# A two-layer windowed transformer: half of a turned input moved to the next step, and one keys' product moved into the projection

## The chip, the cores and the metric

The kernel runs on one core of a Trainium2 chip. The metric is the device time of one execution in microseconds, from start to end of the program. TensorE (PE in the rows) multiplies, DVE is the vector engine, ACT the scalar engine, POOL is GpSimd, SP issues transfers.

## The reference

Eight images of 56 x 56 with 16 channels pass a ReLU and nine 9 x 9 filters each, which gives 160 channels per pixel. Then come two transformer blocks with windows of 7 x 7 pixels and 5 heads of 32, the second with windows shifted by 3 and a mask. A linear layer, a synthesis filter and a 1 x 1 convolution end it. All is float32.

```
for i, (shift, mask) in enumerate(zip(SHIFTS, (None, MASK1))):
    x3 = _swin_block(x3, shift, mask, ...)

# in _swin_block
x = _ln(x, ln1g, ln1b)                       # roll and window partition if shift
q, k, v = split(x @ qkvw + qkvb)
attn = softmax(q @ k.T * HEAD_DIM ** -0.5 + bias + mask)
x = sc + (attn @ v) @ projw + projb
h = _ln(x, ln2g, ln2b)
return x + gelu(h @ w1 + b1) @ w2 + b2
```

## The kernel before

Three phases run one after the other: `phase_a` filters the images, `phase_b` computes both blocks and the linear layer, `phase_c` ends. The change lies in `phase_b`, some 2900 us of the span.

`phase_b` works on strips of 14 rows (two rows of windows), four per image, 32 per layer. Its body is executed once per step `i`, 0 to 63, and once more as prologue and as tail. It is a software pipeline of three strips: attention of strip `i` (parameter `la`, its layer), the MLP of strip `m = i - 1` (`lm`), and the front, that is layer norm and the products Q, K, V, of strip `i + 1` (`ln`). A step with `lm` 0 is called a layer 0 step here (32 of them), one with `lm` 1 a layer 1 step (31, and the tail). Layer 1 steps also compute the last linear layer. Each engine has its own copy of the body, written out by hand, and executes it strictly in that order; semaphores tie them.

Every float32 operand of a matrix product is split in a high part, made by ACT, and a low part, made by DVE as the difference; `split_passes` then multiplies four times (L118). The products of a step, by the names of their uses:

- `T1A0, T1C0, T1A1, T1C1`: TensorE turns the normalised strip z1 (columns 0 to 127 as A, the rest as C; half 0 has four tiles, half 1 three; L1328). `Q0, K0, B0, Q1, K1, B1`: queries, keys, and the fifth head's queries and keys, for halves 0 and 1 of the strip. `V0` to `V3`: values. ACT copies each out; `fifth_head` takes four copies.
- S0 to S3: scores (L1387) of four groups of windows; DVE adds the bias (L1168), takes the maximum (L1175) and the difference (L1178); ACT the exponentials (L997). `OT0` to `OT3`: attention's outputs turned, split by ACT (L1009) and DVE (L1203). `P0, P1, P2`: the projection, of 1, 3 and 3 tiles; DVE adds the residual.
- `T2A0, T2C0, T2A1, T2C1`: z2, the second layer norm's output, turned (L1328) for the MLP, split by `t_hi` on ACT (L1031) and `t_lo` on DVE (L1215) into z2t. `G0` to `G9`: the MLP's first product, five feature blocks for half 0 of the strip, then five for half 1; ACT's gelu (L1040) frees the bank. `W0` to `W5`: its second product (L1441); DVE adds x1b (L1229). `L0` to `L3`: the linear layer from z2t, scaled out by ACT (L1022).

PSUM has two rings whose uses take the banks in turn: `ra` with three banks and `rm` with two. A product waits until the reader has freed the use that had its bank before. A `Ring` is a list of uses in order; the rings PRO, RA and END serve the prologue, the steps and the last step.

TensorE's order at the end of a step was: W3 (layer 1: W4), K1, a wait for OT3's split, P0, P1, B1, P2, V2, S0 of the next strip, W4 and W5 (layer 1: W5, then L0 to L3), T2A0 and T2C0, V3, T2A1 and T2C1. The next step begins with G0 to G4, S1, G5 to G9, S2, W0, T1A0 and T1C0.

DVE's order there: residuals 0 and 1, their statistics and `variance` of half 0, residual 2, `normalise` of half 0 of z2 (L1123), statistics, W4's addition (layer 0), variance of half 1, W5's addition, `normalise` of half 1, `t_lo(0)`, `t_lo(1)`. Next step: the statistics of the strip xa (L1100), the scores' operations for groups 0 and 1, `normalise` of z1.

POOL's body, which the change leaves as it is: `inv_std`, the deviation of the coming strip (L898, eleven small operations); `repeat_rest(z1)` (L904), which copies the rest columns of z1 twice and releases T1; for each half of z2 a power (L928), then `repeat_rest(z2)` (L904), which releases T2 of that half; in layer 1 the linear part's addition to yz (L923); last x1b, in layer 0 seven additions (L936), in layer 1 two passes over the strip (L940, L943).

SP loads the strips xa and xr, and stores xo (layer 0, after W5) or yz (layer 1, after POOL's L923).

Of the kernel before, what the change touches and what calls it, by code (L numbers as in the profile page):

```python
# [17 lines left out]
F32 = mybir.dt.float32  # L18
# [618 lines left out]
def phase_b(nc, keep, xs0, xs1, ys):  # L637
    with ExitStack() as ctx:
# [6 lines left out]
        def bank(name):  # L645
# [53 lines left out]
        FRONT = ["T1A0", "T1C0", "T1A1", "T1C1", "Q0", "K0", "B0", "V0", "Q1", "V1", "K1", "B1", "V2", "V3"]  # L699
        PRO = Ring(FRONT, 3, {})  # L700
        RA = Ring(["T1A0", "T1C0", "T1A1", "T1C1", "OT0", "Q0", "K0", "OT1", "B0", "V0", "Q1", "OT2", "V1", "OT3", "K1",
                   "P0", "P1", "B1", "P2", "V2", "V3"], 3, {})
        END = Ring(["OT0", "OT1", "OT2", "OT3", "P0", "P1", "P2"], 3, {})
# [65 lines left out]
        def t2_half_freed(i, lm):  # L769

            return rm_free[1], m_before(i, lm, M_USES) - 1
# [179 lines left out]
        def _(act):  # L951
            act_ = nc.scalar.activation

            def body(i, la, lm, ln):
# [23 lines left out]
                def fifth_head(hf):  # L978
                    use = f"B{hf}"
                    act.wait_ge(*a_full(i, use))  # L980
                    dims = [[2 * WQ, 4], [1, WT]]
                    for p in range(2):
                        act_(view(q4, p * WP, HD, hf * QH + p * WQ, dims), view(bank_a(i, use), 0, HD, p * WQ, dims), ACT.Copy,
                             scale=float(HD) ** -0.5)
                        last = act_(view(k4, p * WP, HD, hf * QH + p * WQ, dims), view(bank_a(i, use), HD, HD, p * WQ, dims),
                                    ACT.Copy)
                    last.then_inc(a_freed(i, use)[0], 1)

                def values(j):
                    use = f"V{j}"  # L990
                    act.wait_ge(*a_full(i, use))
                    act_(view(vb, 0, QP, j * VJ, [[VW, 2 * HEADS], [1, HD]]),
                         view(bank_a(i, use), 0, QP, 0, [[HD, 2 * HEADS], [1, HD]]), ACT.Copy).then_inc(a_freed(i, use)[0], 1)
# [32 lines left out]
                def t_hi(hf):  # L1026
                    t0, nt = HALF[hf]
                    for part, dst, rows in (("A", z2t[0], 128), ("C", z2t[2], CR)):
                        use = f"T2{part}{hf}"
                        act.wait_ge(*m_full(i, lm, use))  # L1030
                        act_(dst[0:rows, t0 * TT:(t0 + nt) * TT], bank_m(i, lm, use)[0:rows, 0:nt * TT],  # L1031
                             ACT.Copy).then_inc(s_hi2, 1)

                if lm is not None:
                    for g in range(2 * FT):
# [5 lines left out]
                             ACT.Gelu_apprx_tanh).then_inc(m_freed(i, lm, use)[0], 1)  # L1041
                if la is not None:
# [21 lines left out]
                if ln is not None:  # L1064
                    fifth_head(0)
                    values(0)
# [6 lines left out]
                if ln is not None:  # L1073
                    values(1)
# [20 lines left out]
        def _(dve):  # L1095
# [45 lines left out]
            def body(i, la, lm, ln):  # L1141
# [66 lines left out]
                def t_lo(hf):  # L1208
                    t0, nt = HALF[hf]
                    cols = slice(t0 * TT, (t0 + nt) * TT)  # L1210
                    for n, (part, dst, src, rows) in enumerate((("A", z2t[1], z2t[0], slice(0, 128)),
                                                               ("C", z2t[2], z2t[2], slice(REST, 2 * REST)))):
                        use = f"T2{part}{hf}"
                        dve.wait_ge(s_hi2, hi2(i, 2 * hf + n + 1))
                        v.tensor_tensor(dst[rows, cols], bank_m(i, lm, use)[rows, 0:nt * TT], src[rows, cols].bitcast(F32),  # L1215
                                        ALU.subtract).then_inc(m_freed(i, lm, use)[0], 1)
# [60 lines left out]
                if la is not None:  # L1277
# [19 lines left out]
                    residual(2)  # L1297
                    dve.wait_ge(s_pow, 2 * i + 1)
                    normalise(1, z2, x1, *HALF[0])
                    x1_stats(2, True)  # L1300
                if lm == 0:
                    mlp_out(4)
                if la is not None:
                    variance(i, 1)
                if lm is not None:
                    mlp_out(5)
                if la is not None:
                    dve.wait_ge(s_pow, 2 * i + 2)
                    normalise(1, z2, x1, *HALF[1])
                    t_lo(0)  # L1310
                    t_lo(1)
# [5 lines left out]
        def _(pe):  # L1317
# [13 lines left out]
            def body(i, la, lm, ln):  # L1331
# [135 lines left out]
                def mlp_turned(z, name, hf):  # L1467
# [402 lines left out]
```

## Time and profile before

| | us |
|---|---|
| median of 3 runs | 3453.58 |
| lowest, highest | 3445.36, 3461.8 |
| profiled execution | 3450.4 |
| its span, first to last instruction | 3448.9 |
| TensorE busy | 3213.2 (93%) |
| DVE, ACT, POOL busy | 2133.2 (62%), 1779.8 (52%), 908.5 (26%) |
| mean granted TensorE clock | 0.958 |

A row of a timeline has the start and the duration in us, the engine, the line, what is written and read, the shape, the number of instructions merged, and in brackets the idle time before with what ended it. The granted clock is the share of full speed that TensorE was allowed; its two levels are 1.2 and 2.4 GHz. A busy TensorE is not necessarily at its peak.

### The profile page before, as it was taken

The page shows a single profiled execution, that of the slowest core. Times are in us where ns is not written, and L with a number is a line of the kernel's source. Part 1 is how long each engine was busy: PE and PEld are TensorE (multiplying, and loading weights), DVE is VectorE, ACT ScalarE, POOL GpSimd, SP SyncE. Part 2 cuts the span into 40 slices and gives each one's busy share as a digit, 9 for nine tenths or more (in the row PEclk, how much of TensorE's full clock was granted, in tenths as well). Part 3 has the DMA queues.
Part 4 walks back from the last instruction along what each step waited for, and adds up shares of the span by engine and source line. Part 5 has one row for each costly group of instructions (what it writes and reads, how often), then busy time and mean ns, then how long its engine had stood idle before and what let it go on. Part 6 is the DMA issues. An engine that isn't in the chain of part 4 may idle for free. (4 is left out here: it accounts for less than half of the span.)

```text
span 3448.9 us, 103586 instructions
## 1 busy us (share of the span) xinstructions
PE 3213.2 (93%) x40530; PEld 2876.9 (83%) x40530; DVE 2133.2 (62%) x6493; ACT 1779.8 (52%) x4297; POOL 908.5 (26%) x1432
## 2 busy tenths in 40 slices
PE   7996999999999999999999999999999999999689
PEld 6884888888888888888888888888888888888589
DVE  1114677777777777777766666666666666666232
ACT  1111555555555555555555555555656556655221
POOL 5300222222222222222222233322333223332111
PEclk9996899999999999999999999999999999999789
DMA  5321111111111111111111111111111111111275
GB/s 103 94 74 43 30 36 35 35 35 35 35 35 35 35 35 35 35 35 45 44 39 25 36 36 36 30 25 34 36 36 36 28 25 36 36 36 24 51 137 94
DMA packets 246678, 148.38 MB, mean 43 GB/s; under 512 B 31729, under 2 KB 246068, under 8 KB 246586
## 3 DMA queue, kind: packets, MB, share of 16 engines
q1 hardware_dynamic: 244882, 146.95, 18.5%
q0 software_dynamic: 1728, 0.48, 0.1%
q8 instruction: 49, 0.80, 0.1%
q14 instruction: 19, 0.16, 0.0%
HBM read 96.74 MB, written 52.50 MB: 43 GB/s over the span
## 5 line engine op out<-in xcount | busy, mean ns | idle before, releaser
L1441 PE MATMUL rm<-w,ht 128*112 128x160 f32 x4480 | 683.8, 303 | 0.0
L1441 PEld LDWEIGHTS rm<-w,ht 128*112 128x112 f32 x4480 | 610.1, 177 | 9.6 <-ACT ht L1040 0.2
L928 POOL TENSOR_TENSOR rs<-ln_tmp,mhalf 112x4 f32<-112x4 f32 (+1 forms) x128 | 118.9, 929 | 1663.6 <-DVE ln_tmp L1119 1663.6
L1040 ACT ACTIVATE ht<-rm 128x448 f32<-128x448 f32 (+1 forms) x640 | 319.2, 499 | 233.8 <-PE rm L118 231.9
L118 PE MATMUL rm<-z2t_hi,w_hi 128*128 128x448 f32 (+1 forms) x640 | 267.6, 418 | 35.3 <-DVE z2t_lo L1215 34.6
L1168 DVE TENSOR_TENSOR sc<-so,tabs 113x490 f32<-113x490 f32 x256 | 171.2, 669 | 141.2 <-PE so L1387 139.1
L118 PE MATMUL rm<-z2t_lo,w_hi 128*128 128x448 f32 (+1 forms) x640 | 229.2, 358 | 0.0
L118 PE MATMUL rm<-z2t_rest,w_rest 98*128 98x448 f32 (+1 forms) x640 | 228.4, 357 | 0.0
L118 PE MATMUL rm<-z2t_hi,w_lo 128*128 128x448 f32 (+1 forms) x640 | 228.3, 357 | 0.0
L904 POOL TENSOR_TENSOR z<-z,one 112x448 f32<-112x448 f32 (+2 forms) x192 | 131.6, 685 | 367.1 <-DVE z L1123 367.1
L118 PEld LDWEIGHTS rm<-z2t_hi,w_hi 128*128 128x128 f32 x640 | 128.0, 200 | 109.9 <-ACT ht L1040 51.0
L1178 DVE TENSOR_TENSOR sm<-sc,mx 113x490 f32<-113x490 f32 x256 | 174.0, 680 | 37.1 <-ACT pr L997 25.4
L1408 PEld LDWEIGHTS so<-vb,pt 49*49 49x49 f32 x10240 | 142.8, 123 | 60.4 <-issue 55.0
L1328 PE MATMUL rm<-ident,z 112*128 112x112 f32 (+1 forms) x896 | 144.1, 292 | 48.5 <-POOL z L904 32.7
L1185 DVE RECIPROCAL rd<-so 113x10 f32<-113x10 f32 x256 | 56.6, 221 | 208.9 <-PE so L1408 201.1
L1123 DVE TENSOR_SCALAR z<-x,mean,rs 112x160 f32<-112x160 f32 x448 | 133.8, 360 | 80.9 <-POOL rs L928 80.9
L1387 PEld LDWEIGHTS so<-kt,qm 64*49 64x49 f32 x8192 | 141.0, 122 | 49.6 <-issue 44.0
L1009 ACT ACTIVATE ot_hi<-ra 128x98 fp32r<-128x98 f32 x512 | 103.0, 261 | 149.8 <-PE ra L1420 149.8
L1387 PE MATMUL so<-kt,qm 64*49 64x49 f32 x8192 | 172.8, 208 | 1.6 <-DVE sc L1168 1.6
L969 ACT ACTIVATE qm<-ra,qpair 128x400 f32<-128x400 f32 x256 | 138.2, 591 | 69.6 <-PE ra L118 69.6
L1175 DVE TENSOR_REDUCE mx<-sc 113x10 f32<-113x490 f32 x256 | 169.3, 661 | 6.6
L1408 PE MATMUL so<-vb,pt 49*49 49x33 f32 x10240 | 170.3, 210 | 2.8 <-issue 0.9
(244 smaller groups left out, 9300.9 us busy)
## 6 DMA issues: line engine op xcount, KB each, us to landing
xa<-xs SPq DMA_DIRECT2D x128, 245.0 KB
xr<-xs SPq DMA_DIRECT2D x128, 245.0 KB
xs<-a_tok SPq DMA_DIRECT2D x8, 1960.0 KB, 9.5
xs<-xo SPq DMA_DIRECT2D x64, 245.0 KB
ys<-yz SPq DMA_DIRECT2D x64, 245.0 KB
c_y<-ys SPq DMA_DIRECT2D x48, 260.0 KB
c_y<-ys SPq DMA_DIRECT2D x16, 280.0 KB
c_taps<-in_f_syn SPq DMA_DIRECT2D x24, 126.0 KB, 5.1
```

The lines of the kernel that those rows point to most:

```text
L118: last = nc.tensor.matmul(out, lhs, rhs, start=(n == 0), stop=(n == len(pairs) - 1))
L904: gp.tensor_tensor(view(t, 0, TT, t0 * ZW + DIM, [[ZW, nt], [REST, 2], [1, REST]]), once, view(one, 0, TT, 0, [[0, nt], [0, 2], [0, REST]] ...
L969: last = act_(qm[:, odd * QN + hf * QH:odd * QN + (hf + 1) * QH], bank_a(i, use)[:, 0:QH], ACT.Copy, scale=keep.qpair[:, odd:odd + 1])
L1040: act_(ht[:, f * SN + t0 * TT:f * SN + (t0 + nt) * TT], bank_m(i, lm, use)[:, 0:nt * TT], ACT.Gelu_apprx_tanh).then_inc(m_freed(i, lm, use ...
L1123: ins = v.tensor_scalar(z[:, t * ZW:t * ZW + DIM], x_[:, t * DIM:(t + 1) * DIM], mean[n][:, t:t + 1], rs[n][:, t:t + 1], ALU.subtract, ALU ...
L1168: v.tensor_tensor(view(sc, 0, QP, 0, [[SX, 2], [1, SX]]), view(so, 0, QP, 0, [[512, 2], [1, SX]]), tab, ALU.add).then_inc(s_sadd, 1)
L1175: v.tensor_reduce(mx[:], s3, AX.X, ALU.max).then_inc(s_smax, 1)
L1178: v.tensor_tensor(sm[j % 2][:].rearrange("q (g k) -> q g k", k=WT), s3, view(mx, 0, QP, 0, [[1, 2 * HEADS], [0, WT]]), ALU.subtract).then_ ...
L1328: last = tr(bank_of(use)[0:rows, t * TT:(t + 1) * TT], z[:, c:c + rows], keep.ident[0:TT, 0:TT])
L1387: last = mm(so[w * WP:w * WP + WT, row * 512 + b * WT:row * 512 + (b + 1) * WT], q, k, start=True, stop=True)
L1408: last = mm(so[w * WP:w * WP + WT, p * 512 + OC + h * VW:p * 512 + OC + (h + 1) * VW], pt[p * WP:p * WP + WT, h * GK + w * WT:h * GK + (w ...
L1441: last = mm(bank_m(i, lm, use)[0:TT, t * DIM:(t + 1) * DIM], ht[:, c:c + TT], keep.w["w2", lm][:, f * DIM:(f + 1) * DIM], start=(f == 0), ...
```

## The change

Three things. (1) The second half of turned z2 (T2A1, T2C1) is no longer made at the end of step `i`, but in step `i + 1` between G2 and G3, in the `ra` ring instead of `rm`. ACT splits it after gelu G2, DVE after adding the bias of score group 0; TensorE waits for both splits ahead of G5. (2) K1 moves from before P0 to between P1 and P2. (3) B1 goes behind V3 at the end of the step; its copies and V3's go to ACT's next step, behind gelu G2 and gelu G0. Besides, the product W4 (layer 1: W5) and its addition move ahead of V2, and on DVE ahead of the normalisation of half 0, while `t_lo` of half 0 now stands ahead of the normalisation of half 1, not behind it. POOL and SP are unchanged.

```diff
-        RA = Ring([..., "V1", "OT3", "K1",
-                   "P0", "P1", "B1", "P2", "V2", "V3"], 3, {})
+        RA = Ring([..., "V1", "OT3",
+                   "P0", "P1", "K1", "P2", "V2", "V3", "B1", "T2A1", "T2C1"], 3, {})
-        T2 = ["T2A0", "T2C0", "T2A1", "T2C1"]
+        T2 = ["T2A0", "T2C0"]
...
-            return rm_free[1], m_before(i, lm, M_USES) - 1
+            return rm_free[1], m_before(i, lm, M_USES)
+        def turned_full(i, lm, use):
+            return m_full(i, lm, use) if use[-1] == "0" else a_full(i, use)
... ACT
                              ACT.Gelu_apprx_tanh).then_inc(m_freed(i, lm, use)[0], 1)
+                        if g == 0 and la is not None:
+                            values(3, i - 1)
+                        if g == 2:
+                            t_hi(m, 1)
+                            if la is not None:
+                                fifth_head(1, i - 1)
...
                     keys(1)
-                    fifth_head(1)
-                    values(2)
+                    values(2, i)
...
                 if la is not None:
-                    t_hi(0)
-                if ln is not None:
-                    values(3)
-                if la is not None:
-                    t_hi(1)
+                    t_hi(i, 0)
... DVE
                     scores_biased(0, i, la)
+                if lm is not None:
+                    t_lo(m, 1)
+                if la is not None:
                     scores_less_max(0, i)
...
                     residual(2)
+                if lm is not None:
+                    mlp_out(4 + lm)
+                if la is not None:
                     dve.wait_ge(s_pow, 2 * i + 1)
                     normalise(1, z2, x1, *HALF[0])
                     x1_stats(2, True)
                 if lm == 0:
-                    mlp_out(4)
+                    mlp_out(5)
                 if la is not None:
                     variance(i, 1)
-                if lm is not None:
-                    mlp_out(5)
-                if la is not None:
+                    t_lo(i, 0)
                     dve.wait_ge(s_pow, 2 * i + 2)
                     normalise(1, z2, x1, *HALF[1])
-                    t_lo(0)
-                    t_lo(1)
... TensorE
                     pe.wait_ge(*t2_half_freed(i, lm))
-                    mlp_in(range(FT))
+                    mlp_in(range(3))
+                    pe.wait_ge(s_z[1], 2 * m + 2)
+                    mlp_turned(m, 1)
+                    mlp_in(range(3, FT))
                 if la is not None:
                     scores(1, i)
                 if lm is not None:
+                    pe.wait_ge(*a_freed(m, "T2A1"))
+                    pe.wait_ge(*a_freed(m, "T2C1"))
                     mlp_in(range(FT, 2 * FT))
...
-                if ln is not None:
-                    front_product("K", 1)
                 if la is not None:
                     pe.wait_ge(*a_freed(i, "OT3"))
                     projection(0)
                     projection(1)
                 if ln is not None:
-                    front_product("B", 1)
+                    front_product("K", 1)
                 if la is not None:
                     projection(2)
+                if lm is not None:
+                    mlp_out(4 + lm)
                 if ln is not None:
                     values(2)
                     scores(0, i + 1)
                 if lm == 0:
-                    mlp_out(4)
-                if lm is not None:
                     mlp_out(5)
                 if lm == 1:
                     linear(range(4))
                 if la is not None:
                     pe.wait_ge(s_z[1], 2 * i + 1)
-                    mlp_turned(z2, "T2", 0)
+                    mlp_turned(i, 0)
                 if ln is not None:
                     values(3)
-                if la is not None:
-                    pe.wait_ge(s_z[1], 2 * i + 2)
-                    mlp_turned(z2, "T2", 1)
+                    front_product("B", 1)
```

## Rows read from the trace of the kernel before

**Rows 1.** The page, first part: busy time, share of the span and instructions of each engine.

```profile
PE 3213.2 (93%) x40530; PEld 2876.9 (83%) x40530; DVE 2133.2 (62%) x6493; ACT 1779.8 (52%) x4297; POOL 908.5 (26%) x1432
```

**Rows 2.** Windows: 30 layer 0 steps, 27 layer 1 steps, three single steps, the kernel's start.

```profile
core 0: us, PE busy (x) PEld busy (x) DVE busy (x) ACT busy (x) POOL busy (x), PEclk, DMA share, GB/s
422.34:1714.68 1292.34, 1241.73 (x17340) 1111.12 (x17341) 942.85 (x2971) 758.10 (x1861) 322.12 (x661) 0.99 0.15 36
1852.41:3132.89 1280.48, 1229.30 (x16363) 1106.44 (x16363) 859.54 (x2701) 747.29 (x1864) 394.75 (x487) 0.96 0.14 32
1498.17:1542.21 44.04, 42.36 (x579) 38.16 (x579) 31.43 (x100) 25.28 (x63) 10.72 (x23) 0.96 0.14 34
1542.21:1584.98 42.77, 41.09 (x578) 36.69 (x578) 31.42 (x100) 25.26 (x63) 10.71 (x23) 1.00 0.14 35
...
2896.29:2942.65 46.36, 44.37 (x606) 39.67 (x606) 31.83 (x100) 27.64 (x70) 14.61 (x19) 1.00 0.13 33
341.50:352.20 10.70, 7.25 (x96) 6.56 (x100) 6.70 (x16) 4.62 (x12) 0.93 (x1) 0.52 0.22 48
```

**Rows 3.** Waits of TensorE in the 30 layer 0 steps: total us, times, longest.

```profile
PE rm L1328 <- POOL z L904: 27.9, 30, 0.9
PE rm L118 <- DVE z2t_lo L1215: 17.2, 30, 0.7
```

**Rows 4.** Waits of TensorE in the 27 layer 1 steps, the longest in total.

```profile
PE rm L118 <- DVE yz L1229: 28.1, 27, 1.0
```

**Rows 5.** Timeline of a layer 0 step where the projection begins: start us, us.

```profile
1529.00 0.46 PE L118 MATMUL ra<-z1t_hi,qkv_hi 128*128 128x400 f32 x1
1529.09 0.42 DVE L1203 TENSOR_TENSOR ot_rest<-ra,ot_rest 32x98 fp32r<-32x98 f32 x2
...
1529.86 0.24 PE L118 MATMUL ra<-proj_hi,ot_hi 128*112 128x160 f32 x1
```

**Rows 6.** Timeline of TensorE, end of that step: T2A0, G0, G5.

```profile
1537.62 0.55 PE L1328 MATMUL rm<-ident,z 112*128 112x112 f32 x4
...
1542.21 0.47 PE L118 MATMUL rm<-z2t_hi,w_hi 128*128 128x448 f32 x1 [0.58 <-DVE z2t_lo L1215]
...
1547.36 0.42 PE L118 MATMUL rm<-z2t_hi,w_hi 128*128 128x336 f32 x1
```

**Rows 7.** Groups of instructions of ACT: one of the fifth head's two kinds of copy.

```profile
L983 ACT ACTIVATE q<-ra 32x196 f32<-32x196 f32 x256 | 82.0, 320 | 116.2 <-PE ra L118 114.7
```

**Rows 8.** Timeline of a layer 1 step's end: L1 to L3 out, T2A0, split of T2C0, G0.

```profile
2937.65 1.79 ACT L1022 ACTIVATE xo<-rm,std 112x160 f32<-112x160 f32 x5 [1.22 <-PE rm L118]
...
2939.16 0.99 PE L1328 MATMUL rm<-ident,z 112*128 112x112 f32 x8 [0.16 <-ACT xo L1022]
...
2941.04 0.62 DVE L1215 TENSOR_TENSOR z2t_rest<-rm,z2t_rest 32x448 fp32r<-32x448 f32 x1
...
2942.65 0.47 PE L118 MATMUL rm<-z2t_hi,w_hi 128*128 128x448 f32 x1 [0.45 <-DVE z2t_lo L1215]
```

**Rows 9.** Timeline of the same step: DVE's second normalisation, POOL's chain, T1.

```profile
2937.27 0.91 DVE L1123 TENSOR_SCALAR z<-x,mean,rs 112x160 f32<-112x160 f32 x3 [0.73 <-POOL rs L928]
...
2938.26 0.51 POOL L904 TENSOR_TENSOR z<-z,one 112x192 f32<-112x192 f32 x1 [1.02 <-DVE z L1123]
2939.58 2.57 POOL L923 TENSOR_TENSOR yz<-yz,xo 112x1120 f32<-112x1120 f32 x1 [0.81 <-ACT xo L1022]
...
2946.80 0.97 POOL L898 TENSOR_TENSOR ln_tmp<-st 112x7 f32<-112x7 f32 x3
...
2952.79 0.94 POOL L904 TENSOR_TENSOR z<-z,one 112x448 f32<-112x448 f32 x1 [2.12 <-DVE z L1123]
...
2954.99 0.93 PE L1328 MATMUL ra<-ident,z 112*128 112x112 f32 x8
```

**Rows 10.** Timeline of DVE and POOL in the last step with attention.

```profile
3182.68 2.60 POOL L943 TENSOR_TENSOR x1b<-x1b,b 112x1120 f32<-112x1120 f32 x1
...
3183.32 2.49 DVE L1178 TENSOR_TENSOR sm<-sc,mx 113x490 f32<-113x490 f32 x1
```

**Rows 11.** Timeline of TensorE at the kernel's first turn T1 after attention begins.

```profile
344.19 1.75 PE L1328 MATMUL ra<-ident,z 112*128 112x112 f32 x8 [3.45 <-POOL z L904]
...
347.64 1.06 PE L1408 MATMUL so<-vb,pt 49*49 49x33 f32 x40 [0.76 <-ACT pt L1002]
```

More of the change, by code:

```diff
@@ L976, in keys, with fifth_head, values @@
                     act_(kt[:, hf * QH:(hf + 1) * QH], bank_a(i, use)[:, 0:QH], ACT.Copy).then_inc(a_freed(i, use)[0], 1)
[L978 removed]
+                def fifth_head(hf, n):
                     use = f"B{hf}"
[L980 removed]
+                    act.wait_ge(*a_full(n, use))
                     dims = [[2 * WQ, 4], [1, WT]]
                     for p in range(2):
[L983 removed]
+                        act_(view(q4, p * WP, HD, hf * QH + p * WQ, dims), view(bank_a(n, use), 0, HD, p * WQ, dims), ACT.Copy,
                              scale=float(HD) ** -0.5)
[L985 removed]
+                        last = act_(view(k4, p * WP, HD, hf * QH + p * WQ, dims), view(bank_a(n, use), HD, HD, p * WQ, dims),
                                     ACT.Copy)
[L987 to L989 removed]
+                    last.then_inc(a_freed(n, use)[0], 1)
+                def values(j, n):
                     use = f"V{j}"
[L991 removed]
+                    act.wait_ge(*a_full(n, use))
                     act_(view(vb, 0, QP, j * VJ, [[VW, 2 * HEADS], [1, HD]]),
[L993 removed]
+                         view(bank_a(n, use), 0, QP, 0, [[HD, 2 * HEADS], [1, HD]]), ACT.Copy).then_inc(a_freed(n, use)[0], 1)
                 def exps(j):
@@ L1029, in t_hi @@
                         use = f"T2{part}{hf}"
-                        act.wait_ge(*m_full(i, lm, use))
-                        act_(dst[0:rows, t0 * TT:(t0 + nt) * TT], bank_m(i, lm, use)[0:rows, 0:nt * TT],
+                        act.wait_ge(*turned_full(n, lm, use))
+                        act_(dst[0:rows, t0 * TT:(t0 + nt) * TT], turned_bank(n, lm, use)[0:rows, 0:nt * TT],
                              ACT.Copy).then_inc(s_hi2, 1)
@@ L1041, in body @@
                              ACT.Gelu_apprx_tanh).then_inc(m_freed(i, lm, use)[0], 1)
+                        if g == 0 and la is not None:
[4 more added lines that the diff above has]
+                                fifth_head(1, i - 1)
+                elif la is not None:
+                    values(3, i - 1)
+                    fifth_head(1, i - 1)
                 if la is not None:
@@ L1064, in body @@
                 if ln is not None:
[L1065 to L1066 removed]
+                    fifth_head(0, i)
+                    values(0, i)
                 if la is not None:
@@ L1206, in outputs_lo, with t_lo @@
                     ins.then_inc(a_freed(i, use)[0], 1)
-                def t_lo(hf):
+                def t_lo(n, hf):
                     t0, nt = HALF[hf]
                     cols = slice(t0 * TT, (t0 + nt) * TT)
-                    for n, (part, dst, src, rows) in enumerate((("A", z2t[1], z2t[0], slice(0, 128)),
+                    for k, (part, dst, src, rows) in enumerate((("A", z2t[1], z2t[0], slice(0, 128)),
                                                                ("C", z2t[2], z2t[2], slice(REST, 2 * REST)))):
                         use = f"T2{part}{hf}"
-                        dve.wait_ge(s_hi2, hi2(i, 2 * hf + n + 1))
-                        v.tensor_tensor(dst[rows, cols], bank_m(i, lm, use)[rows, 0:nt * TT], src[rows, cols].bitcast(F32),
-                                        ALU.subtract).then_inc(m_freed(i, lm, use)[0], 1)
+                        dve.wait_ge(s_hi2, hi2(n, 2 * hf + k + 1))
+                        v.tensor_tensor(dst[rows, cols], turned_bank(n, lm, use)[rows, 0:nt * TT], src[rows, cols].bitcast(F32),
+                                        ALU.subtract).then_inc(turned_freed(n, lm, use)[0], 1)
                 def mlp_out(n):
```

19 lines of the change are left out of this document (12 added, 7 removed).

## The prediction

> **What bounds the kernel now.** The page comes first: TensorE is busy for 93% of the span and no other engine for over 62% [rows 1], so a microsecond counts where TensorE waits. The windows by stage come next. Thirty layer 0 steps take 1292.34 us, 43.08 each, but one at the full granted clock takes 42.77 and one in which the clock fell takes 44.04; 27 layer 1 steps take 1280.48 us, 47.43 each, against 46.36 at the full clock [rows 2]. So the falls cost 1292.34 - 30 x 42.77 = 9 us in layer 0 and about 1.06 a step in layer 1. The waits of TensorE show three per step and all stand at the step's end [rows 3, 4]: layer 0 waits 0.93 for z2's second half from POOL, 0.57 for its split by DVE and a little for DVE's last addition; layer 1 waits 1.04 for DVE's addition of W5, then a little for ACT's linear copies and for the split. The rest is a chain without gaps.
>
> The change attacks these waits. What matters is what becomes late instead, so I walked one step of each layer through the new orders, engine by engine, with the durations of the timeline (the rows shown are those that carry the sum). Times are those of the step of before; an event "earlier by 1" is so against that step.
>
> **Layer 0.** The start of the projection loses its cover. TensorE ends W3 at 1529.00 and now wants P0 at once; but P0 waits for the split of OT3, which DVE ends at 1529.09 + 0.42 = 1529.51 [rows 5]. K1, 0.86 us long (1529.00 to 1529.86), hid that. P0 starts at 1529.57: a new stall of 0.57, and P0 only 0.29 earlier. From P0 to T2A0 there were 7.76 us (1529.86 to 1537.62); B1 (0.75) leaves and K1 (0.86) enters, so T2A0 stands at 1537.44. DVE's addition of W5 now comes ahead of the second variance: 1537.62 to 1537.94, and T2C0, which needs its bank, starts at 1538.0. Variance 0.83 to 1538.8, the two splits 0.62 each with their small gaps to 1540.1, no longer behind a normalisation of 0.91. TensorE comes from V3 and B1 at 1539.96. G0 starts at 1540.15 instead of 1542.21 [rows 6], 2.06 earlier. Then 0.63 is given back for the six transposes that now stand between G2 and G3; their input is ready at about 1541.7, behind G0 to G2. ACT pays next: after gelu G2 (to 1543.4) it does two splits of 0.45, then the fifth head, four copies of 0.32 to 0.33 [rows 7], to 1545.6, and only then gelu G3 (0.55), which frees G5's bank at 1546.15. TensorE is done with S1 0.5 before. V3's copy hides in ACT's wait for G1. G5 starts at 1546.2 instead of 1547.36. The new wait for T2C1's split ahead of G5 costs nothing: DVE ends it near 1544.9, before S1's end at 1545.7. On DVE the first max and difference of the scores queue behind that split, some 1 us later, and ACT wants them only after its last gelu, past 1550. Nor does POOL come late: its residual additions and statistics bring z1 by 1551.9, and T1 wants it at 1554.42 - 1.15 = 1553.27. So a layer 0 step saves **1.15 us**, 32 of them 37 us. The stalls that remain (0.57, some 0.3, 0.2 and 0.5) lie apart, so I also credit the 9 us of clock falls: -46 in all. Bounds: no credit for the clock and half the gain, -18; the stall at G5 hidden, -62.
>
> **Layer 1, TensorE.** P0 is again 0.29 earlier. W5 is computed and added before the linear layer, so the 1.04 wait for L1 goes. Next late is ACT: each pair of linear tiles takes it 0.68 to 0.72, and with L0 at 2934.34 its five remaining tiles end near 2938.42 instead of 2937.65 + 1.79 = 2939.44. T2A0 starts at 2938.15 instead of 2939.16. Its splits end 1.0 earlier too, at 2940.65 instead of 2941.04 + 0.62 [rows 8], and G0 starts at 2940.72 instead of 2942.65. The same 0.63 and the same wait at G5 follow. TensorE would come to T1 (the turn of z1) at 2954.99 - 1.07 = 2953.9.
>
> **Layer 1, POOL.** Here is the step that I think decides. DVE used to normalise z2's second half at 2937.27, while it waited for T2; now that stands behind the first half's splits, so it starts at 2940.69, 3.42 later. POOL, in its own order, repeats the rest columns of that half (2938.26, now 2941.68), and only then adds the linear part (2.57), makes x1b in two passes (both done by 2946.85) and computes the next strip's deviation (2946.80 to about 2950.7), after which DVE normalises z1 (2.00) and POOL finishes it (2952.79 to 2953.73) [rows 9]. Nothing in that chain had to wait: its only slack was the 0.81 before the linear addition, at 2939.58, and the time from 2953.73 to T1 at 2954.99, which less 0.12 for the semaphore (2940.50 in layer 0's counterpart to its release) leaves 1.14. The addition now starts at 2942.15, **2.57 later**. Without any other effect z1 is turned at 2953.85 + 2.57 = 2956.42, 1.43 later than before. After T1 the step is TensorE's own chain, back to P0, so all of it lengthens the step. (SP stores yz behind the linear addition, so 2.6 later; DVE needs that buffer again with W0's addition, over 8 us on, and xr's load, queued behind the store, is needed half a step later.)
>
> Two corrections have only bounds. POOL's deviation now took 0.97 for three operations of 0.2 each because DVE's L1178 ran over them [rows 9]; without that the chain is 0.43 shorter, a shift of 1.0. The other way, the passes over x1b move to where DVE has both of its L1178 of the step. One L1178 of the trace lasted 2.49 us instead of 0.67, while POOL's L943 ran from 3182.68 to 3185.28 [rows 10]. If both L1178 go between POOL's passes, 2 x 0.67 is added to the 1.0: 2.34. I take the middle, **1.7**, for a step of 48.1 at the full clock, with TensorE standing still for some 2.8 us ahead of T1. The Trainium skill (SBUF — State Buffer, Who interferes with whom) says that a DVE instruction with two SBUF inputs and a GpSimd instruction that reads SBUF exclude each other for a whole instruction, whoever came first; the trace agrees, with the 2.49 us. By that rule alone the shift is 2.34, and the sum below would be 31 x 0.64 = 20 us higher.
>
> **The clock.** A standstill of 2.8 us in one piece is more than any steady step has now; falls came after pieces of 0.93 and 0.57 close together, or of 1.04. After the 3.45 us that TensorE waited for z at the same place in the kernel's first step, the clock was 0.52 from 341.50 to 352.20, that is half, and the eight transposes of T1 took 1.75 instead of 0.93 [rows 2, 11]. From 344.19 to 352.20 there are 8.0 us, 0.76 of them waiting; 7.25 us of work at a rate of 0.53 lose 3.4. So the price of a fall there is up to 3.4; in a layer 0 step it was 1.27 [rows 2]. It may be 0, if none comes. I take **2.0 a step** as a mean over nearly every step having one, nearer to the seen prices than to the largest, as TensorE's half-speed time partly lies in the wait.
>
> **The sum.** Layer 1: 48.1 + 2.0 = 50.1 against 47.43, +2.65 on 31 steps = +82. Layer 0: -46. First and last steps: the same work, taken at nothing (under 3 us either way). 3450.4 + 36 = 3486, made against the profiled execution, which took 3450.4 us around a span of 3448.9; the median of the runs is 3 us above it: **3490 us**, 1.1% slower. A measurement of this kernel tells about 0.5% from no change, 3436 to 3471.
>
> **Rivals.** (1) The clock holds, or falls as seldom as now: 3450.4 - 46 + 31 x 0.67 = 3425, 3428 as a median, faster. For it: idle stretches of 1.0 to 1.6 us per step mostly cost nothing now. Against it: the first steps' fall. It decides when the clock's price in layer 1 is under about 0.3 a step. Chance 0.18, of which some reaches into no change. (2) POOL's chain does not bind, because something in it is shorter than I read it; then layer 1 takes 46.36 - 1.07 = 45.3 without falls, and the total is 3450 - 46 - 66 = 3338. This needs z1 to be 2.1 us earlier than the mildest bound, against durations that repeat to hundredths in every step: 0.07. (3) Both bounds at their worst (2.34, 3.4) and layer 0 gaining only 18: 3450 - 18 + 31 x 4.7 = 3578, or beyond if the low clock lasts: 0.08. (4) The gains and losses cancel, since the price of the clock is near 1 a step: 3455. The waits are moved, and nothing comes of the change: 0.10. The forecast itself, 3471 to 3560, has 0.57.
>
> With these, faster 0.22, no change 0.15, slower 0.63. The range of 8 in 10 is 3415 to 3565: it takes in the forecast, the cancelling case and most of the first rival, and leaves out the second and the worst of the third.
>
> **What the changed profile would show.** Right: no wait of TensorE for POOL's z and DVE's split at the end of layer 0 steps; a wait of about 0.57 before P0 in both layers; 0.3 to 0.6 before G5 for ACT; layer 0 steps of 41.6 us; in layer 1, TensorE's turn of z1 into the ra banks waiting 2 to 3.5 us for POOL L904 in each step, POOL's linear addition starting 2.5 us later against P0, no wait for DVE before L1, and a granted clock under 0.96 in that layer, low just after T1. Wrong: layer 1 steps below 47 us, or a clock near 1.00 there. If layer 0 does not gain, ACT's fifth head or the cover of P0 is what I mis-sized.

## The result and the profile after

The change made the kernel slightly slower: a median of 3465.85 us over six executions (3463.76 to 3474.78) against 3452.18 over six of the kernel before (3444.56 to 3461.8). The ratio is 1.0048 with a 95% interval of [1.0027, 1.0069]: small, but the interval leaves out 1. The forecast was 3490 us, a step of +36 to +38; the measured one is +14.

| | before | after |
|---|---|---|
| profiled execution, us | 3450.4 | 3464.7 |
| its span | 3448.9 | 3462.9 |
| mean granted TensorE clock | 0.958 | 0.961 |

The page of the kernel after, its first part:

```profile
PE 3195.4 (92%) x40530; PEld 2866.0 (83%) x40530; DVE 2158.6 (62%) x6493; ACT 1740.5 (50%) x4297; POOL 921.5 (27%) x1432
```

The same instructions ran, and TensorE is busy 17.8 us less than in [rows 1]. Little can be seen in such a mean, since the two layers went opposite ways. Windows of the kernel after, each from a P0 (the projection's start) to a P0: 32 layer 0 steps, 29 layer 1 steps, one layer 0 step, two layer 1 steps, and 7 us around the start of T1 in the last of them (2616.95). Columns as in [rows 2].

```profile
365.36:1691.32 1325.96, 1300.76 (x18477) 1171.27 (x18477) 1005.16 (x3166) 788.14 (x1984) 349.41 (x704) 1.00 0.15 37
1734.65:3188.96 1454.31, 1333.59 (x17574) 1197.78 (x17575) 948.34 (x2901) 785.50 (x2001) 432.39 (x522) 0.96 0.13 30
1028.30:1069.73 41.43, 40.67 (x578) 36.63 (x579) 31.43 (x100) 24.63 (x62) 10.93 (x22) 1.00 0.14 36
2339.76:2387.97 48.21, 44.04 (x607) 39.50 (x607) 32.70 (x101) 26.92 (x69) 14.91 (x18) 1.00 0.13 32
2588.18:2639.33 51.15, 46.98 (x607) 42.23 (x607) 32.69 (x101) 27.17 (x69) 14.90 (x18) 0.93 0.13 30
2616.00:2623.00 7.00, 6.04 (x59) 5.69 (x63) 3.69 (x7) 2.24 (x4) 0.82 (x1) 0.53 0.35 72
```

And the kernel before, cut at the same places (P0 of the same steps), which [rows 2] are not:

```profile
364.63:1745.13 1380.50, 1324.62 (x18476) 1185.34 (x18477) 1005.19 (x3166) 808.07 (x1984) 343.86 (x704) 0.99 0.14 36
1790.56:3166.66 1376.10, 1320.86 (x17576) 1189.18 (x17574) 923.26 (x2901) 802.73 (x2001) 423.63 (x522) 0.96 0.14 32
```

So layer 0 gained 54.5 us (43.14 to 41.44 a step) and layer 1 lost 78.2 (47.45 to 50.15 a step). A layer 1 step takes 48.21 where the clock held, and 51.15 in the one shown where it fell: there the granted clock is 0.53, near half speed, in the 7 us that begin 0.95 before the wait for z1 ends, and the eight transposes of T1 take 1.75 instead of 0.98. 23 of the 29 steps are longer than 48.35. Of the rest of the difference, the step between the two stretches gained 2.1 (45.43 to 43.33), the last step with attention 0.85 (44.97 to 44.12), and everything behind it 7.45 (3448.9 - 3211.63 = 237.27 to 3462.9 - 3233.08 = 229.82); the start lost 0.7. The sum is -54.5 + 78.2 - 2.1 - 0.85 - 7.45 + 0.7 = +14.0, the difference of the spans. The last 0.7 says nothing: in the profiles of the versions below, whose order up to there is that of the kernel after, the first P0 comes anywhere from 360.43 to 374.29.

Waits of TensorE after, layer 0 stretch (columns as in [rows 3]). The two at the step's end of [rows 3] are gone; the one before P0 and the one before G5 are new:

```profile
PE ra L118 <- DVE ot_rest L1216: 13.4, 33, 1.7
PE rm L118 <- ACT ht L1049: 11.4, 32, 0.4
```

Layer 1 stretch, against [rows 4]:

```profile
PE ra L1343 <- POOL z L913: 83.1, 29, 2.9
PE rm L1343 <- ACT xo L1031: 11.0, 29, 0.5
PE ra L118 <- DVE ot_rest L1216: 10.7, 29, 0.4
PE rm L118 <- ACT ht L1049: 10.1, 29, 0.4
```

83.1 us are waited at the turn of z1, 2.86 in each of 29 steps. The timeline of the layer 1 step from 2339.76 shows how it comes about. DVE:

```profile
2351.17 0.62 DVE L1228 TENSOR_TENSOR z2t_lo<-rm,z2t_hi 128x448 fp32r<-128x448 f32 x1 [3.23 <-ACT z2t_hi L1040]
2351.82 0.62 DVE L1228 TENSOR_TENSOR z2t_rest<-rm,z2t_rest 32x448 fp32r<-32x448 f32 x1
2352.48 0.91 DVE L1136 TENSOR_SCALAR z<-x,mean,rs 112x160 f32<-112x160 f32 x3
...
2358.11 0.97 DVE L1191 TENSOR_TENSOR sm<-sc,mx 113x490 f32<-113x490 f32 x1
...
2360.58 1.48 DVE L1191 TENSOR_TENSOR sm<-sc,mx 113x490 f32<-113x490 f32 x1
...
2365.39 2.00 DVE L1136 TENSOR_SCALAR z<-xa,mean,rs 112x160 f32<-112x160 f32 x7 [3.33 <-POOL rs L907]
```

POOL, in the same stretch:

```profile
2348.01 0.85 POOL L937 TENSOR_TENSOR rs<-ln_tmp,mhalf 112x3 f32<-112x3 f32 x1 [0.96 <-DVE ln_tmp L1132]
2353.46 0.51 POOL L913 TENSOR_TENSOR z<-z,one 112x192 f32<-112x192 f32 x1 [4.60 <-DVE z L1136]
2353.93 2.61 POOL L932 TENSOR_TENSOR yz<-yz,xo 112x1120 f32<-112x1120 f32 x1
2356.48 2.07 POOL L949 TENSOR_TENSOR x1b<-lin_sum,mean 112x1120 f32<-112x1120 f32 x1
2358.63 2.90 POOL L952 TENSOR_TENSOR x1b<-x1b,b 112x1120 f32<-112x1120 f32 x1
2361.49 0.97 POOL L907 TENSOR_TENSOR ln_tmp<-st 112x7 f32<-112x7 f32 x3
...
2367.48 0.93 POOL L913 TENSOR_TENSOR z<-z,one 112x448 f32<-112x448 f32 x1 [2.12 <-DVE z L1136]
```

TensorE:

```profile
2368.54 0.98 PE L1343 MATMUL ra<-ident,z 112*128 112x112 f32 x8 [2.86 <-POOL z L913]
```

The half layer norm's power, which L1136 needs, is ready at 2348.86. DVE then stands idle for 3.23, waiting for ACT, since a split stands before the normalisation in its order. POOL in its turn stands idle for 4.60. From there to 2368.41 POOL works, or waits for DVE's L1136, which itself waits for POOL's statistics: the chain that the prediction followed in [rows 9]. The linear addition (now L932) starts 14.17 after P0 instead of 2939.58 - 2928.22 = 11.36 (2928.22 is P0 of that step in the trace of before), that is 2.81 later.

### The profile page after: what moved, and what is told of

It reads as the page before. It is cut to its first block and busy times, and to the rows that moved or that the text cites. A ratio compares the mean times of both kernels' runs of the same rounds, so it can differ in the third digit from the quotient of the medians.

```text
span 3462.9 us, 104230 instructions
## 1 busy us (share of the span) xinstructions
PE 3195.4 (92%) x40530; PEld 2866.0 (83%) x40530; DVE 2158.6 (62%) x6493; ACT 1740.5 (50%) x4297; POOL 921.5 (27%) x1432
## 5 line engine op out<-in xcount | busy, mean ns | idle before, releaser
L1456 PE MATMUL rm<-w,ht 128*112 128x160 f32 x4480 | 715.6, 311 | 0.0
L1456 PEld LDWEIGHTS rm<-w,ht 128*112 128x112 f32 x4480 | 636.8, 183 | 8.0 <-ACT ht L1049 0.2
L1343 PE MATMUL ra<-ident,z 112*128 112x112 f32 (+1 forms) x1280 | 176.0, 281 | 109.2 <-POOL z L913 109.2
L1343 PEld LDWEIGHTS ra<-ident,z 112*128 112x128 f32 (+1 forms) x1280 | 142.9, 144 | 125.3 <-issue 112.9
L971 ACT ACTIVATE z1t_hi<-ra 128x448 fp32r<-128x448 f32 (+1 forms) x128 | 68.2, 533 | 308.8 <-PE ra L1343 308.8
L1191 DVE TENSOR_TENSOR sm<-sc,mx 113x490 f32<-113x490 f32 x256 | 205.6, 803 | 16.3 <-ACT pr L1006 1.0
L1181 DVE TENSOR_TENSOR sc<-so,tabs 113x490 f32<-113x490 f32 x256 | 170.9, 668 | 53.7 <-PE so L1402 45.1
L1001 ACT ACTIVATE vb<-ra 113x320 f32<-113x320 f32 x256 | 112.8, 441 | 179.6 <-PE ra L118 178.1
L1136 DVE TENSOR_SCALAR z<-xa,mean,rs 112x160 f32<-112x160 f32 x448 | 128.1, 358 | 113.8 <-POOL rs L907 113.8
L985 ACT ACTIVATE kt<-ra 128x400 f32<-128x400 f32 x128 | 64.6, 504 | 244.1 <-PE ra L118 244.1
L1411 PE MATMUL pt_ps<-gather,pr 113*128 113x113 f32 x1280 | 181.2, 275 | 0.7 <-ACT pr L1006 0.7
```

Source lines behind the costliest of these rows:

```text
L1136: ins = v.tensor_scalar(z[:, t * ZW:t * ZW + DIM], x_[:, t * DIM:(t + 1) * DIM], mean[n][:, t:t + 1], rs[n][:, t:t + 1], ALU.subtract, ALU ...
L1181: v.tensor_tensor(view(sc, 0, QP, 0, [[SX, 2], [1, SX]]), view(so, 0, QP, 0, [[512, 2], [1, SX]]), tab, ALU.add).then_inc(s_sadd, 1)
L1191: v.tensor_tensor(sm[j % 2][:].rearrange("q (g k) -> q g k", k=WT), s3, view(mx, 0, QP, 0, [[1, 2 * HEADS], [0, WT]]), ALU.subtract).then_ ...
L1343: last = tr(bank_of(use)[0:rows, t * TT:(t + 1) * TT], z[:, c:c + rows], keep.ident[0:TT, 0:TT])
L1411: last = tr(pt_ps[:, h * GK:h * GK + QP], pr[j % 2][:, SLOT[h] * 2 * WP:(SLOT[h] + 1) * 2 * WP], gather[:])
L1456: last = mm(bank_m(i, lm, use)[0:TT, t * DIM:(t + 1) * DIM], ht[:, c:c + TT], keep.w["w2", lm][:, f * DIM:(f + 1) * DIM], start=(f == 0), ...
```

## The experiments

The theory (A): z1 comes late because L1136 of z2's second half stands behind the first half's split on DVE, which is DVE's order alone; the wait that follows in turn costs clock. Rivals: POOL's chain is too long whatever DVE does (port conflicts with DVE, or x1b itself); or the clock falls because of the many new gaps of all the engines' queues, not because of that one wait. The two with the normalisation first, the one with 17 products and K1 alone ran on one chip, beside 16 executions of the kernel before with a median of 3451.63; the other four on another, beside 7 with 3454.46. Ratios are to these.

**The normalisation first, in layer 1 only.** From the changed kernel, on DVE:

```diff
                     variance(i, 1)
-                    t_lo(i, 0)
+                    if lm != 1:
+                        t_lo(i, 0)
                     dve.wait_ge(s_pow, 2 * i + 2)
                     normalise(1, z2, x1, *HALF[1])
+                    if lm == 1:
+                        t_lo(i, 0)
```

> The changed kernel, with one edit: in layer 1 steps DVE normalises z2's second half before it splits the turned first half, as in the kernel before. Theory A (POOL's chain is late because of that normalisation's place, and the clock falls because TensorE stands still ahead of T1): the wait of 2.86 us for POOL's z goes, POOL's linear addition then starts at ACT's last linear copy, and the step at the full clock falls from 48.2 to about 45.4 us; no falls are left in layer 1, so 29 steps of 50.15 become 45.4 and the total drops by about 135 us, to some 3330. Theory B (the chain is bound by something else, the shared port or ACT's linear copies): POOL's chain starts at most 1 us earlier, the wait keeps over half of its length, total 3400 to 3450. Theory C (the falls have another cause than the standstill): step 45.4 at the full clock, but a granted clock of still about 0.96 in layer 1, total about 3390.

3321.75 us (3313.76 to 3326.93), ratio 0.9634 [0.9605, 0.9663]: 144 us below the median of the kernel after. One layer 1 step and 28 of them in its windows:

```profile
2456.38:2501.51 45.13, 43.84 (x606) 39.52 (x607) 31.76 (x101) 26.92 (x69) 14.58 (x18) 1.00 0.15 34
1779.38:3043.10 1263.72, 1227.36 (x16968) 1106.79 (x16969) 889.56 (x2801) 753.67 (x1932) 408.38 (x504) 1.00 0.14 34
```

Every layer 1 step takes 45.13, the clock is 1.00 throughout, and the waits of TensorE in these 28 steps no longer hold POOL's z:

```profile
PE rm L1346 <- ACT xo L1031: 10.6, 28, 0.4
PE ra L118 <- DVE ot_rest L1216: 10.4, 28, 0.4
PE rm L118 <- ACT ht L1049: 9.8, 28, 0.4
```

POOL in the step from 2456.38:

```profile
2464.62 0.85 POOL L937 TENSOR_TENSOR rs<-ln_tmp,mhalf 112x3 f32<-112x3 f32 x1 [0.95 <-DVE ln_tmp L1132]
2466.50 0.51 POOL L913 TENSOR_TENSOR z<-z,one 112x192 f32<-112x192 f32 x1 [1.02 <-DVE z L1136]
2466.97 2.58 POOL L932 TENSOR_TENSOR yz<-yz,xo 112x1120 f32<-112x1120 f32 x1
...
2471.64 2.60 POOL L952 TENSOR_TENSOR x1b<-x1b,b 112x1120 f32<-112x1120 f32 x1
```

The linear addition starts 10.59 after P0 instead of 14.17. So the chain moved up by 3.58, more than the wait of 2.86, and its length didn't bind. The first part of (A) stands: the order on DVE alone cost 48.20 - 45.13 = 3.07 a step at the full clock, and 1.95 more through the clock. The swap of the two lines, not the move of the second half of z2, is what made this change a loss.

**The same swap in both layers.**

```diff
                     variance(i, 1)
-                    t_lo(i, 0)
                     dve.wait_ge(s_pow, 2 * i + 2)
                     normalise(1, z2, x1, *HALF[1])
+                    t_lo(i, 0)
```

> The changed kernel with the same edit in both layers. Theory A expects layer 1 as in the run beside it. In layer 0, DVE has the second variance behind W5's addition, so the normalisation waits for POOL's power and the splits of the turned first half come about 1.8 us later; G0 is then late by 1.5 to 1.9 us, and the layer 0 step goes from 41.43 to 43.0 to 43.3, at or above the 42.77 of the kernel before: total some 50 to 60 us above the run with the edit in layer 1 alone. The rival, that the order on DVE costs nothing in layer 0, because G0's wait moves into waits that are there anyway: step of 41.4 to 41.8.

3417.98 us (3415.95 to 3425.74), 0.9913 [0.9889, 0.9937], so 96 us worse than with the swap in layer 1 alone. Layer 1 is as good (45.1); layer 0, in 32 steps, is

```profile
374.29:1792.88 1418.59, 1340.49 (x18476) 1202.73 (x18476) 1007.43 (x3166) 788.94 (x1984) 331.56 (x704) 0.97 0.14 35
```

44.33 a step instead of 41.44. Its largest wait of TensorE, and where it comes from on DVE in one step:

```profile
PE rm L118 <- DVE z2t_rest L1228: 53.8, 32, 1.7
```

```profile
916.67 0.91 DVE L1136 TENSOR_SCALAR z<-x,mean,rs 112x160 f32<-112x160 f32 x3 [0.97 <-POOL rs L937]
917.49 0.62 DVE L1228 TENSOR_TENSOR z2t_lo<-rm,z2t_hi 128x448 fp32r<-128x448 f32 x1
918.14 0.62 DVE L1228 TENSOR_TENSOR z2t_rest<-rm,z2t_rest 32x448 fp32r<-32x448 f32 x1
```

Here there is no linear layer between the variance and T2, so DVE waits 0.97 for POOL's power and spends 0.91 while G0 already wants the split. G0 waits 1.69 in every step. At the full clock the step is 43.31, 1.88 longer; the clock, which fell in 24 of 32 steps, adds 1.0 on the mean. The same two lines are right in one order in layer 0 and in the other in layer 1.

**The wait kept, but filled with work.** To separate the clock from the wait, layer 1 steps of the changed kernel compute products that no result uses while z1 is still on its way:

```diff
                     mlp_out(0)
+                if lm == 1 and la is not None and ln is not None:
+                    pe.wait_ge(s_pte, i * NG)
+                    for n in range(17):
+                        mm(pt_ps[0:TT, 0:DIM], ht[:, 0:TT], keep.w["w2", lm][:, 0:DIM], start=True, stop=True)
                 if ln is not None:
                     front_turned(0)
```

> The changed kernel, with work added that no result uses: in layer 1 steps, between W0 and the turn of z1, TensorE multiplies 17 more times as in W0, about 2.4 us, into a bank that is free. Theory A (the falls of the clock come from the standstill): the wait for POOL's z shrinks to about 0.5 us, the clock in layer 1 stays at 1.00, every such step takes 48.2 to 48.3 instead of 50.15, and the whole kernel is about 55 us faster than the changed one, in spite of more work: some 3410. Theory C (the falls have another cause, such as the thin products behind the turn): clock still about 0.96, steps of about 50.2, total as the changed kernel or above.

3460.53 us (3454.07 to 3465.43), 1.0027 [1.0004, 1.0051]. The total was missed, and the trace says why: each product is two instructions, and the 34 take longer than the wait they were to fill.

```profile
2319.91 4.78 PE L1505 MATMUL pt_ps<-w,ht 128*112 128x160 f32 x34
2324.53 0.93 PE L1343 MATMUL ra<-ident,z 112*128 112x112 f32 x8
```

T1 starts 4.62 behind the first of them, where the wait had been 2.86. It comes 30.38 after P0 instead of 28.78, so the step is 49.76 at the full clock. The clock itself answers the question: 1.00 over the 28 steps. With ten products instead of 17:

> The changed kernel with 10 products of work that no result uses in place of 17. The run before gave each product two instructions of 0.14 us on TensorE, so 17 took 4.6 us, more than the wait of 2.86 they were to fill; 10 take 2.75. The falls of the clock were gone with 17 (none in layer 1, 23 in the changed kernel). If the standstill is their cause, they stay away and the step is the one at the full clock, 48.2 us, which is 1.9 below the changed kernel's mean of 50.15 on 29 steps: total about 55 us below the changed kernel, 3410. If only the larger amount of work kept them away, falls come back and the total is 3440 to 3465.

Three executions took 3406.22, 3409.16 and 3419.37 us, a ratio of 0.9878 [0.9838, 0.9918]. A fourth took 4761.92 at a mean granted clock of 0.599; it has no profile, and why stays open. Window of 28 layer 1 steps, and T1 of one:

```profile
1780.15:3129.80 1349.65, 1309.38 (x17529) 1181.69 (x17529) 915.40 (x2801) 753.71 (x1932) 417.01 (x504) 1.00 0.14 31
```

```profile
2336.13 2.88 PE L1505 MATMUL pt_ps<-w,ht 128*112 128x160 f32 x20
2339.13 0.98 PE L1343 MATMUL ra<-ident,z 112*128 112x112 f32 x8
```

T1 comes when it did (28.77 after P0), the step is the 48.20 of a step without a fall, and there is no fall: 1349.65 / 28 = 48.20. Against the changed kernel 50.15 - 48.20 = 1.95 a step are gone by giving TensorE more to do. Every other engine's order and z1's time are as they were, so the new gaps in the other queues are not the cause. That settles the second part of (A): it is TensorE's standstill before T1 that the clock answers to, and its price was 1.95 a step on the mean, 57 us in 29 steps.

**K1 moved alone.** From the kernel before, K1 goes between P1 and B1, and nothing else changes:

```diff
-        RA = Ring([..., "OT3", "K1",
-                   "P0", "P1", "B1", "P2", "V2", "V3"], 3, {})
+        RA = Ring([..., "OT3",
+                   "P0", "P1", "K1", "B1", "P2", "V2", "V3"], 3, {})
...
-                if ln is not None:
-                    front_product("K", 1)
                 if la is not None:
                     pe.wait_ge(*a_freed(i, "OT3"))
...
                 if ln is not None:
+                    front_product("K", 1)
                     front_product("B", 1)
```

> The kernel before, with one part of the change alone: K1 between P1 and P2, ahead of B1. My theory: the cover of P0 is gone, TensorE waits 0.37 us for the split of OT3 in every step, as in the changed kernel; nothing is won, since z2's second half at the step's end hangs on DVE and POOL, which come 0.4 to 0.5 us earlier with P0 and P1 but 0.1 to 0.4 later with P2: layer 0 step 42.5 to 43.1 against 42.77, layer 1 46.4 to 46.8 against 46.37, total within 15 us of the kernel before. The rival, that starting the projection earlier is the gain of the change: steps shorter by 0.4 or more in both layers, total 3425 or less.

3440.48 us (3429.89 to 3448.06), 0.9966 [0.9949, 0.9983]: 11 us faster than before, a step as small as that of the whole change, the other way. In layer 1 it helps (46.17 a step without falls, against 47.45 with them in 11 of 29), as the wait for yz shrinks from [rows 4]:

```profile
PE rm L118 <- DVE yz L1229: 5.8, 28, 0.2
```

In layer 0 it shortens the wait for POOL's z from 0.93 to 0.56, opens one of 0.30 before P0, and takes 42.90 where the clock held; but the clock now fell in 24 of 32 steps, not in 8 (with the first step in both), and the mean is 44.0 against 43.14. The falls were not in the expectation. K1 alone thus cost layer 0 27.5 us (1408.03 against 1380.50), of which 0.13 x 32 = 4 are not the clock's:

```profile
360.68:1768.71 1408.03, 1358.45 (x18476) 1207.97 (x18476) 1012.60 (x3166) 807.48 (x1984) 343.09 (x704) 0.97 0.14 35
```

**K1 back ahead of P0**, on top of the first experiment (ring order "OT3", "K1", "P0", "P1", "P2"):

```diff
                     mlp_out(3 + lm)
+                if ln is not None:
+                    front_product("K", 1)
                 if la is not None:
                     pe.wait_ge(*a_freed(i, "OT3"))
                     projection(0)
                     projection(1)
-                if ln is not None:
-                    front_product("K", 1)
-                if la is not None:
                     projection(2)
```

> The version with the early normalisation in layer 1, and K1 ahead of P0 again, in TensorE's order and in the ring. Theory: the move of K1 brings nothing in this order; with K1 back the wait of 0.37 before P0 is gone, in layer 1 the step falls from 45.13 to 44.8, and in layer 0 little changes (41.2 to 41.5 against 41.43), since z2's first half then comes 0.5 later and T2A0 waits for it: total 8 to 15 us below the version it stands on. The rival, that starting the projection early carries the gain: steps longer by 0.3 or more, total above it by 15 or more.

3305.46 us (3303.94 to 3306.46), 0.9563 [0.9536, 0.9591]. 31 layer 0 steps and 28 of layer 1:

```profile
407.92:1682.47 1274.55, 1258.62 (x17919) 1134.28 (x17918) 977.60 (x3069) 759.21 (x1922) 336.90 (x682) 1.00 0.15 38
1770.41:3028.57 1258.16, 1225.73 (x16970) 1105.56 (x16968) 891.57 (x2801) 753.20 (x1932) 422.20 (x504) 1.00 0.15 34
```

41.11 instead of 41.43, and 44.93 instead of 45.13. (The first step, left out here, is longer: 42.44 instead of 41.40.) The wait before P0 is gone in both. In layer 1 part of it comes back before T1, where POOL's chain is now just the last to arrive:

```profile
PE ra L1346 <- POOL z L913: 6.3, 28, 0.2
```

So K1's place between the projections, one of the three things of the change, cost 0.32 a step in layer 0 and 0.20 in layer 1, and K1 covers the split of OT3 better where it was.

**The fifth head's copies behind gelu G3**, so that G5's bank comes free sooner (on top of the first experiment, and then on top of the last):

```diff
                         if g == 2:
                             t_hi(m, 1)
-                            if la is not None:
-                                fifth_head(1, i - 1)
+                        if g == 3 and la is not None:
+                            fifth_head(1, i - 1)
```

> The version with the early normalisation in layer 1, and the fifth head's four copies behind gelu G3 in place of gelu G2 on ACT. G5 waits 0.36 in every step for gelu G3, which stands behind those copies; with G3's gelu first the wait goes, gelu G4 is done just as G6 wants its bank, and both layers' steps fall by 0.30 to 0.36 us: total about 20 us below the version it stands on. If the wait only moves to G6, steps stay as they are.

3318.4 us (3314.33 to 3321.12), 0.9597 [0.9569, 0.9625]: not to be told from the 0.9634 without it. The expected 20 us did not come. G5 no longer waits, but the gelu of G4 now does, behind the four copies, and with it the bank of G6:

```profile
1051.92 0.42 PE L118 MATMUL rm<-z2t_hi,w_hi 128*128 128x336 f32 x1 [0.18 <-ACT ht L1049]
```

A wait of 0.18 for one of 0.36, steps of 41.31 and 45.01 instead of 41.43 and 45.13: 0.12 each, 7 us in all by the steps.

> The two edits together on the version with the early normalisation. If they touch different waits their gains add: layer 1 step 44.4 to 44.5, layer 0 step 40.9 to 41.1, total about 3290. If K1's return only moves the wait in layer 0, the total is that of the version with the copies behind gelu G3 minus 10.

3305.53 us (3300.56 to 3309.17), 0.9567 [0.954, 0.9595], the same as with K1 back alone and 15 above the expected 3290: the gains do not add. In layer 0 the 0.13 is there (40.98 against 41.11); in layer 1 it goes into the wait before T1 (0.37 instead of 0.22), and the step stays at 44.96. The best version is the change with the normalisation first in layer 1 and K1 left where it was: 4.4% faster than the kernel before. Which of the change's other parts wins layer 0's time (the moved half of z2, B1's new place, the earlier W4 and W5) was not run apart; K1's move is not it, since it alone made the layer 0 step 0.13 longer at the full clock.

## Why the prediction was right in direction and wrong in size

- **Layer 1: right, with luck in two sizes.** "The addition now starts at 2942.15, 2.57 later", with P0 0.29 earlier: 2.86 against P0, measured 2.81. The step was put at 48.1 at the full clock and "some 2.8 us" of standstill before T1; measured are 48.20 and 2.86. The 0.12 "for the semaphore" holds too (the release at "2940.50" is a slip for 1540.50, of layer 0); after, POOL ends at 2368.41 and T1 starts at 2368.54. But the 1.7 between the bounds came near by luck, as neither correction came as worked out. The 0.43 that the deviation's first operations were to save was not saved (0.97 again, at 2361.49), and the passes over x1b grew by 0.30 (L952 2.90 instead of 2.60), not by twice 0.67: of the two L1191, one delayed POOL, and the other started under a pass of POOL's and was itself delayed. That makes 1.43 + 0.30 = 1.73, against a measured 48.20 - 46.37 = 1.83. The clock's price, "2.0 a step", is 1.95, and the version with ten products shows it to be the standstill's. It is a mean of 23 steps with a fall, at 2.5 each, and 6 with none, where the prediction gave nearly every step one of 2.0.
- **"+2.65 on 31 steps = +82": two steps too many.** 29 steps have the wait, and their sum is +78.2. The step that carries layer 0 into layer 1 waits only 0.40 at T1 and gained 2.1; the last one has no T1 and gained 0.85. For these two the prediction had put +5.3.
- **Layer 0, "1.15 us" and "-46": mis-sized.** A step at the full clock went from 42.77 to 41.43, 1.34. The missing 0.2 is not at P0, which came later than put: W3's last ten instructions start 2.11 before P0 in the kernel before (1527.75 to 1529.86) and 1.90 before it after (1026.40 to 1028.30), so P0 is 0.21 earlier, not 0.29. (The view's wait of 0.37 counts from the end of the last of them, the "new stall of 0.57" from where K1 had started.) It lies between P0 and G5. G0 was put 10.58 behind P0 (1540.15 - 1529.57) and came 10.43 behind it (1038.73); G5 was put 16.63 behind it and came 16.40 behind it (1044.70), since ACT's gelu G3 ended at 1044.57, 0.3 sooner than put. Of the 32 steps the prediction credited 37 + 9; measured are 1.34 x 32 = 42.9 at the full clock and 11.6 for what lay above it before (falls in 7 steps, and a first step of 45.43), 54.5 in all. "So I also credit the 9 us of clock falls" was right in kind: behind the first step not one fall is left in layer 0.
- **"First and last steps: the same work, taken at nothing (under 3 us either way)": failed.** What lies behind the last P0 took 7.45 less, more than the 3 allowed. The granted clock in its first 33 us was 0.80 before and 1.00 after (kernel before, then kernel after):

```profile
3211.63:3245.00 33.37, 28.74 (x168) 26.00 (x169) 10.93 (x41) 10.69 (x22) 10.15 (x7) 0.80 0.07 17
```

```profile
3233.08:3266.00 32.92, 29.72 (x218) 27.45 (x218) 11.81 (x44) 12.60 (x29) 10.66 (x8) 1.00 0.07 17
```

The window of after is 0.45 shorter and holds 50 more matrix instructions. The longest wait of TensorE there, before and after:

```profile
3220.10 0.47 PE L118 MATMUL rm<-lin_hi,z2t_hi 128*112 128x160 f32 x1 [3.34 <-DVE yz L1229]
```

```profile
3243.41 0.47 PE L118 MATMUL rm<-z2t_hi,w_hi 128*128 128x448 f32 x1 [1.56 <-DVE z2t_rest L1228]
```

The first is the wait of [rows 4] for W5's addition, 3.34 here instead of 1.04, with a clock of 0.51 in the 13 us behind it. The prediction took it out of the layer 1 steps ("W5 is computed and added before the linear layer, so the 1.04 wait for L1 goes") and forgot it in the last one. This is not where the clock happened to fall: from the last P0 to the end of the span it is 237.3 before and 235.7 with K1 alone, which both have the 3.34, and 229.8 to 231.7 in all eight profiles with W5 moved, of which all but that of the kernel after do have a low spell there. The order of W5 was not tried by itself.

So the step that failed is the sum of the gains, in three of its terms; the mechanism was right. Layer 0 won 8.5 more than put, the two steps counted with the 29 came 8.25 lower, and the work behind them 7.45, where nothing was put. Less 1.35 for the 29 steps, which lost that much more than 2.65 each, and 0.7 at the start, that is the 22 us between 36 and 14. No term is off by much, but +14 is what is left of gains of 64.9 and a loss of 78.2, and 46 of gains had been forecast.

- **The rivals.** That the clock holds (3428) did not happen, but the version with ten products is that case, with 3409 in the middle of its three: lower by 19, of which layer 0 and the work behind the last P0 are about 15. That POOL's chain does not bind (3338) is what the first experiment made true, with 3322. The case in which gains and losses cancel (3455) was given 0.10 for the wrong reason, a clock price near 1; the price was 2, and the cancelling came from layer 0, the two steps and the end.

## What to carry over

When an instruction of a hand-written order waits for another engine, ask what stands ready behind it, and do so for each stage that shares the code: here one line above or below another was worth 3.07 us a step at the full clock in layer 1 and -1.88 in layer 0. Follow the chain through the slack of the engine behind (POOL was 26% busy and still bound the layer), and count the clock as part of a standstill's price. When a forecast is the small difference of two large terms, the terms taken "at nothing" deserve as much care as the ones that are summed.

## What was not expected of the hardware

The clock does not follow the sum of the waits. The first step of layer 0 has a low spell in every version and is left out here. Layer 0 of the kernel before stands still for about 1.7 us a step in three pieces (0.93, 0.57 and a little) and fell in 7 of 31 steps; with K1 moved alone it stands still for about 1.4 (0.56, 0.57, 0.30) and fell in 23 of 31. With 1.69 in one piece beside two of 0.36 it fell in 23 of 31. In layer 1 it fell in 11 of 29 steps with 1.04, 0.5 and a little, and in 23 of 29 with 2.86 in one piece and three of 0.36 to 0.38. It fell in no layer 1 step of K1 alone, with 0.45 and three smaller pieces, 1.1 in all, and in no steady step of the versions whose waits are one to three pieces of at most 0.38. What distinguishes the steps that fall from those of the same kernel that don't stays open.

The lock between DVE and POOL works both ways in one step. The first L1191 of that timeline began while POOL's L949 still ran (to 2358.55) and took 0.97 instead of 0.67; L952 began at 2358.63 within it and took 2.90 instead of 2.60; the second L1191 began at 2360.58 under L952 and took 1.48. The Trainium skill says so (SBUF — State Buffer, Who interferes with whom): two SBUF inputs on DVE and a read by GpSimd exclude each other for an instruction, whoever is first. The trace agrees, with these durations. Over the whole kernel L1191 averaged 803 ns after the change and 673 with the normalisation first in layer 1, as its page shows:

```profile
L1191 DVE TENSOR_TENSOR sm<-sc,mx 113x490 f32<-113x490 f32 x256 | 172.2, 673 | 16.8 <-ACT pr L1006 1.5
```

The 3.58 by which POOL's passes moved took them from under DVE's scores. That shortened L952 by 0.3, a small part of the 3.07.
